# A recurrent attention and mixture-of-experts block on one core: silus of the last blocks, the tail's warming products, and the position steps put in another order

## The reference

```python
x = L0_attn_x                                  # (16, 256, 128)
xn = _layernorm(x, axis=-1)
s = _L0_attn_ref(xn, ...)                      # mLSTM-like attention, 4 heads of 32
g = _silu(_L0_ffn_ref(xn, ...))                # 8 experts, each token takes its top one
x = x + s * g
```

## Time and profile before

| What | Value |
|---|---|
| Median of 3 runs | 235.09 us (234.85 to 235.75) |
| Profiled execution | 235.47 us |
| Its span | 233.7 us |
| TensorE products busy | 217.2 us, 93% |
| VectorE busy | 162.4 us, 69% |
| ScalarE busy | 140.3 us, 60% |
| GpSimd busy | 92.6 us, 40% |
| Mean granted clock of TensorE | 0.985 |

### The profile page before, as it was taken

How to read it: one execution, slowest core, us unless ns; L and a number is a source line. 1 busy time by engine, 2 the same in 40 slices (tenths; PEclk the granted TensorE clock), 3 DMA queues, 4 the chain that set the end, 5 groups by cost and what they waited for, 6 DMA issues and landing times.

```text
span 233.7 us, 6082 instructions
## 1 busy us (share of the span) xinstructions
PE 217.2 (93%) x1824; PEld 173.1 (74%) x1834; DVE 162.4 (69%) x491; ACT 140.3 (60%) x326; POOL 92.6 (40%) x130
## 2 busy tenths in 40 slices
PE   8998989678899889999999999999999999998994
PEld 6787654234545454569999999999999999996541
DVE  5998699507467658755877987798779967963170
ACT  2398758456767676877556655665566555552044
POOL 5667930756566563000333333333433333335100
PEclk9999999976999999999999999999999999999999
DMA  6999999930179111400077021011101001000498
GB/s 180 328 363 418 337 205 210 209 111 34 49 202 327 35 48 44 129 3 28 18 223 255 14 67 57 23 57 56 47 28 52 22 26 35 17 22 13 110 341 267
DMA packets 23617, 29.26 MB, mean 125 GB/s; under 512 B 3319, under 2 KB 18687, under 8 KB 23585
## 3 DMA queue, kind: packets, MB, share of 16 engines
q1 hardware_dynamic: 18994, 20.42, 26.5%
q0 software_dynamic: 3424, 8.36, 14.5%
q10 hardware_dynamic: 1168, 0.10, 0.4%
HBM read 19.99 MB, written 9.34 MB: 126 GB/s over the span
## 4 chain that ended last, share of the span: by engine, by line
PE 73%; DVE 13%; issue 5%; ACT 2%; another core or an unknown queue 2%; DMA 2%; POOL 0%; DVEq 0%; SPq 0%; ACTq 0%
PE bank L1213 15%; PE bank L1222 15%; PE head_bank L1213 15%; PE head_bank L1171 5%; PE bank L1183 4%; DVE cm L876 4%; PE bank L1161 3%; DVE stats L711 2%; PE bank L1199 2%; PE head_bank L1141 2%; PE bank L1285 2%; DMA x_sb<-in_L_attn_x 2%; PE bank L1288 1%; PE head_bank L1285 1%
## 5 line engine op out<-in xcount | busy, mean ns | idle before, releaser
L450 POOL DMA_INDIRECT y_tokens<-ffn,idx x39 | 38.6, 991 | 88.1 <-DVE ffn L1004 87.5
L876 DVE TENSOR_TENSOR cm<-dm,head_bank 128x1024 f32<-128x1024 f32 (+1 forms) x32 | 29.1, 951 | 23.7 <-PE head_bank L1171 8.5
L444 POOL DMA_INDIRECT xs_sorted<-xn,pos x32 | 31.1, 973 | 28.0 <-PE head_bank L1171 10.5
L1222 PE MATMUL bank<-w_sb,dm 128*128 x312 | 41.3, 275 | 0.1
L1213 PE MATMUL bank<-xsT,wc 128*128 128x128 f32 x320 | 39.0, 275 | 0.0
L1222 PEld LDWEIGHTS bank<-w_sb,dm 128*128 128x128 f32 x312 | 38.0, 192 | 0.3 <-issue 0.3
L1213 PEld LDWEIGHTS bank<-xsT,wc 128*128 128x128 f32 x320 | 37.3, 192 | 0.0
L1213 PE MATMUL head_bank<-xsT,wc 128*128 128x128 f32 x304 | 37.0, 275 | 0.0
L1213 PEld LDWEIGHTS head_bank<-xsT,wc 128*128 128x128 f32 x304 | 35.5, 192 | 0.0
L586 ACT ACTIVATE wc<-w_sb 128x512 f32 x39 | 24.6, 630 | 14.4 <-issue 14.3
L565 ACT ACTIVATE dm<-bank 128x512 f32<-128x512 f32 x48 | 27.0, 597 | 8.1 <-PE bank L1161 7.5
(11 more groups left out here) (192 smaller groups left out, 345.5 us busy)
## 6 DMA issues: line engine op xcount, KB each, us to landing
x_sb<-in_L_attn_x SPq DMA_DIRECT2D x16, 256.0 KB, 5.1
w_sb<-in_L_ffn_w SPq DMA_DIRECT2D x8, 512.0 KB, 8.9
w_sb<-negated_rows POOLq DMA_DIRECT2D x8, 508.0 KB
xs_sb<-xs_sorted SPq DMA_DIRECT2D x13, 192.0 KB
xs_sorted<-b_sb SPq DMA_DIRECT2D x1, 2048.0 KB, 11.1
w_sb<-y_tokens SPq DMA_DIRECT2D x8, 256.0 KB, 4.4
out_x<-w_sb SPq DMA_DIRECT2D x8, 256.0 KB, 2.5
y_tokens<-ffn,idx POOLq DMA_INDIRECT x39, 2.3
```

Source lines behind the costliest of these rows:

```text
L444: pool.indirect_dma_start(xs_dram, bass.IndirectOffsetOnAxis(ap=pos[:, t:t + 1], axis=0), xn[:, t, :], None).then_inc(s_scat, 16)
L450: pool.indirect_dma_start(y_dram, bass.IndirectOffsetOnAxis(ap=idx[:, j:j + 1], axis=0), ys_sb[:, j // CH % 2, j % CH, :], None, bounds_ch ...
L876: dve.tensor_tensor(cm[:, b % 2, :, m0:m1, :], dm[:, b % 2, :, m0:m1, :], head_bank[:, :, m0 * P:m1 * P].rearrange("p h (m t) -> p h m t", ...
L1222: last = pe.matmul(bank[6 + j % 2][:, 0:D], uT[:, j % 2, c, :], w2_sb[:, bass.ds(e * (HC * D) + c * D, D)], start=(c == 0), stop=(c == HC ...
```

## The change

Five places. (1) In the last iterations of the expert loop (j = 38 on), sigmoid(36) stands ahead of gate(38) on ScalarE and silu(j-2) ahead of product(j) and add_bias(j-1) on VectorE, without a normalisation step behind it. (2) TensorE's six products of zeros in the tail are gone. (3) token_rows(14) and outputs(14) stand behind hidden(0) and gate(0). (4) Of the position steps only the first (L846) stays ahead of weigh(0); reduction and conversion follow it. (5) left_rows(2) also follows weigh(0).

```diff
@@ scalar engine
+            def sigmoid(j):
+                act.wait_ge(s_yb, j + 1)
+                if j >= 2:
+                    act.wait_ge(s_ye, j - 1)
+                act.activation(sy[:, j % 2, :], yb[:, j % 2, :], ACT.Sigmoid).then_inc(s_sy, 1)
...
                 if b == B - 1:
                     act.wait_ge(s_cm, 2 * (B - 1))
                     gate(0)
+                    outputs(b - 1)
...
-                if b + 1 < B:
+                if b + 2 < B:
                     outputs(b)
...
+                if j == NBLK - 1:
+                    sigmoid(j - 2)
                 if 1 <= j < NBLK:
                     gate(j)
                 if j == 1:
                     outputs(B - 1)
-                if j >= 2:
-                    act.wait_ge(s_yb, j - 1)
-                    if j >= 4:
-                        act.wait_ge(s_ye, j - 3)
-                    act.activation(sy[:, j % 2, :], yb[:, j % 2, :], ACT.Sigmoid).then_inc(s_sy, 1)
+                if j >= 2 and j != NBLK - 1:
+                    sigmoid(j - 2)
@@ vector engine
-                for place in positions():
-                    link(place)
+                places = positions()
+                link(next(places))
                 dve.tensor_scalar(left[:, 1, :], ...).then_inc(s_lf1, 1)
-                left_rows(2)
                 for b in range(B):
                     weigh(b)
+                    if b == 0:
+                        for place in places:
+                            link(place)
+                        left_rows(2)
...
+                if j >= NBLK - 1:
+                    silu(j - 2)
                 if 1 <= j < NBLK:
                     product(j)
...
                 if 1 <= j <= NBLK:
                     add_bias(j - 1)
-                if j >= 2:
+                if 2 <= j < NBLK - 1:
                     silu(j - 2)
                     step(normals)
@@ tensor engine
                     pe.wait_ge(s_dm, 3 * B)
                     hidden(0)
+                    token_rows(b - 1)
...
-                if b + 1 < B:
+                if b + 2 < B:
                     token_rows(b)
...
             for g in range(NPC):
-                if g == NPC - 1:
-                    keep_warm(6, g)
                 pe.matmul(bank[g][:, :], ident[:, :], x_sb[:, g * TP:(g + 1) * TP, :], start=True, stop=False)
```

## The result

The changed kernel is slower: a median of 239.31 us (238.4 to 240.21) against 235.42 for the kernel before on the same chip (234.85 to 237.16), a ratio of 1.0153 with an interval of 1.0076 to 1.0229. Forecast were 233.3 us and a range of 231.9 to 234.5. The profiled execution took 240.21 us, with a span of 238.4.

The account below looks back on a forecast made before the run. It took TensorE alone as the bound from about 106 to 211 us, with TensorE and VectorE waiting on each other before and the tail after; -0.50 - 0.71 - 0.6 + 0 = -1.8 took 235.09 to 233.3 us, range 231.9 to 234.5.

Parts of the forecast that it names:

- `token_rows(14)`, -0.50: Start of the experts: hidden(0) fills TensorE's idle wait for ScalarE's copy of uTs, so later blocks come 0.50 us sooner.
- Silus, -0.71: Last expert blocks: earlier silus start the last scatter of y 0.71 us sooner, though bias(38) comes 0.25 later.
- No warming, -0.6: Tail: without six warming products the y sums start earlier, worth 0.6 us, between 0 and 0.8.
- the tail is bound by its transfers: Rival, tail: removing the warming is worth nothing, gain 1.2 us, total 233.9; chance 0.13.
- The front, 0, with ends of -0.55 and +0.6: Attention's start: position steps behind weigh(0) change the total by 0; at best -0.55 us, at worst +0.6 from a new wait.
- The stall of 3.07 us: Attention, at 44.69 us: TensorE and VectorE idle; taken to end with the large transfers at 47.8, unmoved by the change.
- The clock falls in the tail's sums: Rival, tail: TensorE's clock drops to 1.2 GHz during the y sums, adding 3.4 us, total 237.3; chance 0.04.
- The change does little: Rival, front: a new wait there takes back 1 us, total 234.3; chance 0.09.
- The front gain stays: Rival, front: the stall follows a fixed amount of work, so the earlier weighing's gain of up to 0.55 counts, 232.8; chance 0.17.

Follow-up runs that it names:

- e15: The kernel before with only the silus and sigmoids of the last blocks moved; 235.73 us, ratio 1.0004.
- e14: The kernel before with only the six warming products of the tail removed; 235.43 us, ratio 0.9983.
- e12: The changed kernel with the position steps and left_rows(2) back ahead of weigh(0) and the six warming products back; 235.50 us, ratio 0.9996.
- e1: The kernel before with only the later position steps and left_rows(2) moved behind weigh(0); 240.50 us, ratio 1.0189.
- e11: The kernel before with only the 0.18 us conversion to `pos` moved behind weigh(0); 238.95 us, ratio 1.0110.
- e4: The kernel before without its 32 row scatters, so the sorted rows are missing; 222.86 us in one run.
- e5: The kernel before with each row scatter replaced by a plain copy of the same tile, issued by GpSimd; 223.11 us in one run.
- e3: The kernel before with all 32 row scatters held until three `scores` are done and packed into ten images; 243.13 us, ratio 1.0294.
- e7: The kernel before with each row scatter replaced by a plain copy of the same tile, issued by SyncE; 222.86 us in one run.
- e6: The kernel before with each row scatter replaced by two sums on GpSimd, no transfer; 223.13 us in one run.
- e9: The changed kernel with parts (4) and (5) undone and row scatters paced from count 1, at most three a `scores`; 231.18 us, ratio 0.9780.
- e10: The changed kernel, all parts kept, with row scatters paced from count 1, at most three a `scores`; 230.69 us, ratio 0.9785.

## Why the prediction was wrong

Point by point, by its steps.

*`token_rows(14)`, -0.50.* Right. From weigh(15) to hidden(1) it was 4.76 us before (101.02 to 105.78) and is 4.20 now (106.61 to 110.81), -0.56, and the transposes follow hidden(0) with no wait. The experts pass it on.

*Silus, -0.71.* The mechanism was right, the size off, the value small. The last scatter starts 0.52 earlier. bias(38) is indeed late, but by 0.49 against hidden(38) (4.82 us behind its first product instead of 4.33), where I had 0.25: bias(37) comes 0.25 late too (217.38, 0.39 us behind the signal of down(37) at 216.99, where it was 0.15; the runs don't show why), and both then add up. And I had counted the gain of the scatters as a gain of the end while counting the warming's room separately. By e15 the 0.52 don't reach the end at all when TensorE bounds the sums.

*No warming, -0.6.* The direction was right: -0.77 in e14, and 1.0 on average against e12. With a spread of 1.9 us between such tails, that 0.77 lies inside my 0 to -0.8 is partly luck. In the changed kernel itself the time from load to end was +0.09: the last sum 0.32 sooner, the last store 0.41 later. Such a late store, 3.49 to 3.66 us behind the last sum, stands in four of the six kernels without warming and in none with it (3.22 to 3.23), which is the rival "the tail is bound by its transfers", in part. That stores held the loads is not shown: the last three products start 7.13 to 8.91 us behind the first load in those six and 7.22 to 8.04 in the others, and the 8.16 here is hardly outside. By the rule of the Trainium skill, "DMA: Bandwidth & Descriptors", section "Two DMAs through the same engine are not ordered", that within one queue of one engine descriptors start in order (but are pipelined), the term would be 0.8; e14 with 0.77 is near it and the changed kernel's own tail with +0.09 is not, and neither decides, within that spread.

*The front, 0, with ends of -0.55 and +0.6.* This is the step that failed, and it measured +4.20 (+3.54 alone in e1, +4.21 by the later `pos` alone in e11). weigh(0) itself did as I said: from the first product of scores(0) it starts 1.54 us on instead of 2.50, -0.96 (I had 0.95), and scores(1) ends 3.99 instead of 4.80 behind scores(0). What failed is the sentence on the side: "Eight row scatters start later, but the rest wait for `scores`, and the last ends 10 us before its blocks are needed at 101: cost nothing". I asked when the scatters were needed and not what they do to the others while they run. The stall of 3.07 us that I laid on the large transfers, because both ended at 47.8, is theirs: without scatters it is gone (e4), while with plain copies of the same bytes beside the same large loads it is gone too (e5). The end of the stall and that of the transfers at 47.8 were a coincidence. The rows for the right reading were in the trace of before: images of 3.23 and 4.65 us in turn, with two and three scatters, and a weighing that starts 2.24 us behind products of 0.94.

*The rivals.* "The clock falls in the tail's sums" was wrong in kind: the x sums end at 226.49, the first y sum starts at 226.57, and the clock is 1.00 until 238.31, behind the last sums. "The change does little" had the right place, a new wait in front, and a price of 1 us where it was 4.2. "The front gain stays" has its 0.96 and loses it to the stall. So the forecast's sign hung on a term that I had bounded by the length of the moved instructions, when the engine to look at was the one they release.

The parts of the profiled difference: +1.40 of chance ahead of scores(0), +4.20 in the attention, -1.08 + 0.18 + 0.09 = -0.81 in the rest, together the 4.8 us between the two spans; the medians differ by 3.9.

One number of the forecast does not come out of its own terms: the lower end of the range, 231.9, was to be the front rival with its terms at their best, and 235.09 - 0.50 - 0.96 - 0.8 - 0.55 gives 232.3. It doesn't matter beside 4.20.

## What to carry to other kernels

When an instruction is moved, ask not only who waits for its result but what it starts, and when that will run against the others. Where scatters of single rows by GpSimd run beside a chain of TensorE and its readers, try them spread out, two for each round of some 3 us and never many back to back; a wait on the chain's own counter does it, and it must hold from the first scatter. Here a wait that the profile laid on "issue" or on something remote, behind products whose row had long ended, was their sign: compare rounds with different numbers of such scatters before laying such a wait on the bandwidth.

## What the runs showed of the hardware

- Row scatters of 128 rows, 0.97 us each and 0.30 between two, delay what waits for TensorE. Two in a round of 3.20 us cost 0.03, three 1.45, four 2.78 (once, in e3; seven in a run made a round of 8.54 there). In a run of ten a result of 0.94 us of products was read 5.7 us after their start, and one of 0.86 us 10.0 us after. Single ones, 2.79 us apart in the experts' stage, cost nothing that shows: TensorE is busy for 99.00 of the 99 us from 106 to 205 before, beside 33 of them.
- Plain copies of 64 KB a tile by GpSimd or SyncE (e5, e7), and sums of 0.5 us end to end on GpSimd (e6), cost the attention under 0.1 us against e4.
- The granted clock fell from 2.4 to 1.2 GHz in the attention of every profiled execution with a stall in front (after at 54.0, TensorE busy 1.50 of the 4 us at 48 to 52) and not once in the attentions of e4 to e7, e9 and e10. In seven of 56 executions of the kernel before the mean clock was 1.00 all the same.
- A register read in front of an add on VectorE keeps its least length of about 0.8 us, from the start of the instruction ahead to that of the add, also when that instruction is a silu: bias(38) starts 0.83 behind the start of silu(37) (218.12 to 218.95).
